# The opening of an image tower's mixer in its own instruction order, and the class token's gates and routing moved

## Time and profile before

| | |
|---|---|
| Median of 3 runs | 1067.86 us (1067.56 to 1068.58) |
| The profiled execution | 1067.47 us, its span 1065.7 us |
| Busy share of the span | TensorE 91%, VectorE 66%, ScalarE 43%, GpSimd 35% |
| Mean granted TensorE clock | 0.955 |
| Steps 0 to 3 and step 4 up to its shared expert | 0 to 132 us |
| The rest of the mixer's steps | 132 to about 608 us |

### The profile page before, as it was taken

The page is one execution under the profiler, slowest core; times in us unless marked ns, Lnnn a source line. Parts: engine busy times, 40 slices in busy tenths (PEclk is TensorE's granted clock), DMA queues, the critical chain, the costliest instruction groups (busy, mean ns, idle before and its releaser), DMA issues.

```text
span 1065.7 us, 21605 instructions
## 1 busy us (share of the span) xinstructions
PE 970.7 (91%) x6889; PEld 899.1 (84%) x6890; DVE 705.3 (66%) x2095; ACT 454.7 (43%) x1139; POOL 378.0 (35%) x468
## 2 busy tenths in 40 slices
PE   5787788999999999999788999999999999999995
PEld 3555587888888888888787899999999999999995
DVE  3458788887887877888776446464645546564643
ACT  2011143344444444444332255555555555555553
POOL 4232554242343243343421133443243424243222
PEclk9667799999999999999999799999999999999998
DMA  9300610111100111100011372837272633664322
GB/s 275 104 10 11 173 40 1 40 42 40 40 20 22 38 40 40 40 20 15 32 45 41 122 202 45 208 52 190 40 212 45 168 79 80 163 129 126 45 40 31
DMA packets 48164, 82.68 MB, mean 78 GB/s; under 512 B 6416, under 2 KB 30883, under 8 KB 48132
## 3 DMA queue, kind: packets, MB, share of 16 engines
q0 software_dynamic: 31056, 57.46, 22.3%
q1 hardware_dynamic: 17076, 24.84, 7.9%
HBM read 55.32 MB, written 26.96 MB: 77 GB/s over the span
## 4 chain that ended last, share of the span: by engine, by line
PE 41%; issue 27%; DVE 15%; POOL 13%; ACT 1%; POOLq 1%; DMA 0%; DVEq 0%; SPq 0%; ACTq 0%
PE ps_nd L657 14%; PE ps_proj L642 8%; POOL out L603 5%; PE ps_proj L722 5%; PE ps_ri L642 4%; DVE rden L1254 3%; PE ps_ip L642 3%; POOL v_rows L498 2%; PE ps_nd L843 2%; POOL h L561 1%; PE ps_h L830 1%; PE ps_h L815 1%; POOL rstd L494 1%; PE ps_t L729 1%; DVE A L1386 1%
## 5 line engine op out<-in xcount | busy, mean ns | idle before, releaser
L1077 DVE TENSOR_TENSOR GL<-g_act,GH 128x256 fp32r<-128x256 f32 (+1 forms) x424 | 185.3, 439 | 189.4 <-ACT GH L955 170.3
L657 PE MATMUL ps_nd<-w2h,GH 128*128 128x256 f32 x832 | 248.9, 299 | 24.9 <-DVE GL L1077 13.5
L950 ACT ACTIVATE g_act<-ps_proj,fcb 128x256 f32<-128x256 f32 (+1 forms) x280 | 130.8, 468 | 308.8 <-PE ps_proj L642 300.6
L657 PE MATMUL ps_nd<-w2l,GH 128*128 128x256 f32 x832 | 235.8, 283 | 0.0
L657 PE MATMUL ps_nd<-w2h,GL 128*128 128x256 f32 x832 | 234.7, 282 | 0.0
L657 PEld LDWEIGHTS ps_nd<-w2h,GH 128*128 128x128 f32 x832 | 158.4, 190 | 35.2 <-DVE GL L1077 14.0
L955 ACT CAST GH<-g_act 128x256 fp32r<-128x256 f32 x416 | 161.4, 397 | 0.0
L657 PEld LDWEIGHTS ps_nd<-w2l,GH 128*128 128x128 f32 x832 | 158.8, 191 | 0.0
L657 PEld LDWEIGHTS ps_nd<-w2h,GL 128*128 128x128 f32 x832 | 158.1, 190 | 0.0
L642 PE MATMUL ps_proj<-xh,w1h 128*128 128x256 f32 x544 | 116.3, 295 | 9.3 <-issue 4.4
L603 POOL DMA_INDIRECT out<-yb,rows_to x72 | 114.8, 1595 | 16.7 <-issue 12.8
(11 more groups left out here) (271 smaller groups left out, 1943.4 us busy)
## 6 DMA issues: line engine op xcount, KB each, us to landing
R<-v_rows SPq DMA_DIRECT2D x37, 260.0 KB
w1h<-fc_w POOLq DMA_DIRECT2D x9, 1024.0 KB
w2h<-pj_w POOLq DMA_DIRECT2D x9, 1024.0 KB
stage<-fc_w POOLq DMA_DIRECT2D x9, 1024.0 KB
stage<-pj_w POOLq DMA_DIRECT2D x9, 1024.0 KB
v_rows<-tail_rows SPq DMA_DIRECT2D x16, 260.0 KB, 3.0
x<-x SPq DMA_DIRECT2D x16, 256.0 KB, 3.6
out<-yb SPq DMA_DIRECT2D x16, 256.0 KB, 2.1
```

Source lines behind the costliest of these rows:

```text
L657: last = pe.matmul(banks[a], g[:, j, a * P:(a + 1) * P], w[i][:, j, :], start=(j == 0 and q == 0), stop=(j == HT - 1 and q == 2))
L950: act.activation(g_act[:, j % G_SLOTS, 0:width], banks[j % len(banks)][:, 0:width], ACT.Gelu_apprx_tanh, bias=fcb[i][:, j:j + 1]).then_inc ...
L1077: dve.tensor_tensor(GL[:, j, 0:width], g_act[:, j % G_SLOTS, 0:width], GH[:, j, 0:width].bitcast(F32), ALU.subtract).then_inc(gl_done, 1)
```

## The change

Steps 0 to 3 no longer use `step` but a function `opening` of each engine, with an order of their own. The parts of step became functions with names, and step calls them in the same order as before. In `steps`:

```diff
-        def steps(step):
+        def steps(opening, step):
             def over(eng):
                 for t in range(PEEL):
-                    step(t, t % 2)
+                    (opening if t < DEPTH - 1 else step)(t, t % 2)
```

ScalarE's opening follows the same order (tanh of the gates ahead of the projections' copies of steps 2 and 3). The class token's gates, in cls_a of TensorE, in fp32 on the weights as loaded:

```diff
-                pe.wait_ge(gate_w_split, 6)
-                pe.wait_ge(cls_dve, 4)
+                pe.wait_ge(gate_w_loaded, 48)
+                pe.wait_ge(cls_act, 1)
                 for i in range(3):
                     for e in range(FT):
-                        dst = ps_ri[:, i // 2, ((i % 2) * FT + e) * 2:((i % 2) * FT + e) * 2 + 2]
-                        last = split_product(pe, dst, (gates_h[i], gates_l[i]),
-                                             slice(e * P, (e + 1) * P), (c_uh, c_ul))
+                        c = (i % 2) * FT + e
+                        for k in range(FT):
+                            last = pe.matmul(ps_ri[:, i // 2, c:c + 1],
+                                             gates_raw[i][:, k, e * P:(e + 1) * P], c_ut[:, k:k + 1],
+                                             start=(k == 0), stop=(k == FT - 1))
```

```diff
                 if live(t - 4):
                     n = t - 4
+                    if isinstance(n, int) and n == 1:
+                        cls_d()
                     pe.wait_ge(vl_done, n + 1)
-                    pe.wait_ge(run_ready, n + 1)
+                    if not (isinstance(n, int) and n == 0):
+                        pe.wait_ge(run_ready, n + 1)
```

More of the change, by code:

```diff
@@ L391, in step @@
                     store_base(sp, t - 5)
-            return step
+            return opening, step
         def experts_sync(sp):
@@ L664, in mixer_tensor, with columns @@
         def mixer_tensor(pe):
-            def columns(row, dst):
+            def columns(row, dst, copies):
                 for k in range(FT):
-                    for c in range(2):
-                        last = pe.matmul(dst[:, 2 * k + c:2 * k + c + 1],
+                    for c in range(copies):
+                        last = pe.matmul(dst[:, copies * k + c:copies * k + c + 1],
                                          row[0:1, k * P:(k + 1) * P], ones_pp[0:1, 0:1],
@@ L782, in ranks, with transpose_y, scan_out @@
                 last.then_inc(rank_ready, 1)
+            def transpose_y(n):
+                if isinstance(n, int) and n == 0:
+                    pe.wait_ge(consts, CONSTS)
+                pe.wait_ge(y_ready, n + 1)
+                after(pe, ul_done, n)
+                transposes(Y).then_inc(yT_ps, 1)
+            def scan_out(n):
+                if isinstance(n, int) and n == 0:
+                    pe.wait_ge(cls_row1, 1)
+                pe.wait_ge(scan_done, FT * (n + 1))
+                pe.wait_ge(hx_done, at_most(n + 2, NIMG))
+                for lt in range(LT):
+                    for k in range(FT):
+                        last = pe.matmul(ps_h[:, lt, :], HS[:, k, lt * P:(lt + 1) * P],
+                                         wout_sb[:, k, :], start=(k == 0), stop=(k == FT - 1))
+                last.then_inc(attn_ready, 1)
@@ new lines, in y_out @@
+            def y_out(n):
+                if isinstance(n, int) and n == 0:
+                    pe.wait_ge(w_loaded, 16 * W_LOADS)
+                pe.wait_ge(yT_sb, n + 1)
+                after(pe, h1_done, n - 1)
+                for lt in range(LT):
+                    for f in range(FT):
+                        last = pe.matmul(ps_h[:, lt, :], YT[:, f, lt * P:(lt + 1) * P],
+                                         outw_sb[:, f, :], start=(f == 0),
+                                         stop=(f == FT - 1))
+                    last.then_inc(h_ready, 1)
@@ new lines, in numerators @@
+            def numerators(n):
+                if isinstance(n, int) and n == 0:
+                    pe.wait_ge(prep_act, 1)
+                pe.wait_ge(ekv_done, LT * (n + 1))
+                after(pe, t1_done, LT * n)
+                after(pe, y_done, 2 * (n - 4))
+                for tt in range(LT):
+                    for s in range(LT):
+                        last = pe.matmul(ps_nd[:, tt, :], ewT[:, s, tt * P:(tt + 1) * P],
+                                         E[:, s, :], start=(s == 0), stop=(s == LT - 1))
+                    last.then_inc(nd_ready, 1)
@@ L809, in step @@
                 if live(t - 3):
[L810 to L817, removed]
+                    scan_out(t - 3)
                 if live(t):
@@ L820, in step @@
                 if live(t - 1):
[L821 to L833, removed]
-                if live(t):
[L835 to L845, removed]
+                    y_out(t - 1)
+                if live(t):
+                    numerators(t)
                 n = t - 4
@@ L1001, in step @@
                 if live(t - 1):
[L1002 to L1010, removed]
+                    copy_y(t - 1)
                 if live(t):
                     exp_and_tanh(t, par, 1)
[L1013 to L1016, removed]
                 if live(t - 4) and live(t):
@@ L1404, in step @@
                 shared(t - 4, range(6, 7))
                 if live(t - 2):
[L1406 to L1411 removed]
+                    scan(t - 2)
                 shared(t - 4, range(7, 8))
```

490 lines of the change are left out of this document (314 added, 176 removed).

## The result

| | before | changed |
|---|---|---|
| Median, us | 1067.71 (1067.48 to 1068.58, 4 runs) | 1059.03 (1057.70 to 1060.27, 4 runs) |
| Ratio | | 0.9915, 95% interval 0.9902 to 0.9929 |
| The profiled execution | 1067.47, span 1065.7 | 1057.70, span 1055.9 |
| First matmul of the shared expert, step 4 | 131.99 | 113.43 |
| The same, step 5 | 167.00 | 157.16 |

Faster by 8.7 us where 3.5 were forecast, and 0.5 us outside the range. In the profiled pair the opening gained 18.56 us (12.9 forecast), and 8.7 of them went again between the end of step 4's products and step 5's shared expert (9.4 forecast). The remaining 9.8 us stay nearly whole to the end.

What follows compares the result with a forecast made beforehand. TensorE bounds the kernel from 132 to 560 us, waits bound the opening. Opening -12.9 and class routing between steps 4 and 5 +9.4 give -3.5 us: 1064.4 beside 1067.86; range 1059.5 to 1070.5, the forecast's own 1062 to 1067.

Steps and rivals of the forecast that it cites:

- the opening: First 132 us, up to step 4's shared expert: bound by waits, to be shortened by 12.9 us.
- The new chain: Steps 1 to 3 reordered: older image's U ahead of younger's numerators; step 4's transposes at 109.1 instead of 118.95.
- The loss between steps 4 and 5: Class routing there holds TensorE's routing matmuls of image 1: 6.4 us, plus 3.0 for the low clock, 9.4 together.
- the cover: Step 1: class gates and project(1,1) lie beside the making of U(0), at 39.6; gates 2.7 us, at most 5.6.
- rival A: Step 3: scan_out(0) at full clock, 2.0 not 3.8 us, gates 2.1 not 3.4; another 3.3, 1061.1 us; chance 0.20.
- the entry into step 4: From step 4's transposes to its shared expert at full clock: 10.0 instead of 13.04 us, another 3.0 gained.
- the two stretches from residual to U: Making U of one image in the opening: 9.1 us instead of 10.55, waits behind reciprocals gone.
- B: Step 5: the clock holds over the class pause; 3.0 us more gain, 1061.4 us; chance 0.08.
- C: Step 3's numerators don't bring back the full clock; the 3.0 us at step 4's entry stay, 1067.4; chance 0.08.
- E: TensorE stays at 1.2 GHz through step 2, from step 1's numerators on; 7.6 us later, 1072.0; chance 0.12.
- D: Step 1's class gates take 10.4 us; U(0) and all behind it 5.7 later, 1070.1 us; chance 0.06.

Runs made afterwards that it cites:

- 2 + 8 + 8 + 3: Changed kernel with unused 512-column matmuls: 2 in step 1 before U(0), 8 in each wait for U(1) and U(2), 3 in step 5; ratio 0.9859 to before.
- 8 + 8: Changed kernel with 8 unused 512-column matmuls in each of the two stretches where TensorE waits for U(1) and U(2); ratio 0.9845 to before.
- 8 + 8 + 3: Changed kernel with 8 unused matmuls in each wait for U(1) and U(2), and 3 in step 5 behind the class token's total; ratio 0.9849 to before.
- The filler: Unused 512-column matmuls added to the changed kernel in TensorE's waits; 16 in each of two waits left 32 records in 13.90 us, time 1070.68 us.
- old-order run: Changed kernel with the order of steps 0 to 3 as before on every engine, class token's work left in its new place; ratio 0.9959 to before.

## Why the prediction was wrong in size

**What held.** The new chain went as written: output product at 26.90, U's transposes at 38.24, 62.42 and 93.46 (39.6, 65.0 and 98.9 forecast), step 4's transposes waiting for Y(3). The loss between steps 4 and 5 was 8.7 us for 9.4: 6.1 of chain, then the low clock (2.5). From step 5 on all was earlier by 9.5 to 9.8 us. The gate matmuls took the 2.7 us of the forecast by luck: its 0.23 was a record at the low clock, and a one-column matmul leaves two records (the 12 left 24), so at that clock it would have been some 5.5 us. The full clock halved it (0.11 a record). Both stay under the cover, so nothing hung on it. The chain's links and place are shown by the runs with fewer links and with the chain elsewhere, and the order's share of the gain by the run without it.

**The step that failed** is the clock within the numerators after each wait for U. The prediction left six of their eight records at the low rate, 6.1 to 6.5 us in all. They took 4.86, 4.71 and 4.56, because the clock was full again after the first few. The same group stood in the trace of the kernel before, also out of a wait, in 5.16:

```profile
17.08 5.16 PE L843 MATMUL ps_nd<-E,ewT 128*128 128x512 f32 x8 [1.56 <-DVE E L1247]
```

The earlier trace rows has its first four records (3.46), so the other four took 1.7; the prediction added 2.6 for them. From U to Y it forecast 9.8 to 10.2 us, and 8.8, 8.65 and 8.5 were measured, 4.2 less in the three steps. The shorter numerators account for all of it: the prediction's own form, the end of the numerators plus 2.7 for Y, gives 0.3 us less than was measured in each step. The 0.3 is VectorE's, which the chain of waits shows: it takes its two halves of 1.76 and 1.66 one behind the other from the first half of the numerators on, and the second half of the numerators lies beside the first of these. In step 1 Y(1) (47.03) wasn't on the path at all; TensorE reached its transposes at 47.93, behind the gates and the projection. The run with 2 + 8 + 8 + 3 shows the term from the other side: with the clock up the numerators take 3.60 in all three steps.

Three more stretches were shorter than the working had them. The output product of image 0 ran at the full clock (1.97 us, not 3.8; 1.4 us in the start of U(0)). From Y(1) to the end of image 1's product it took 4.6 us, not 5.5. From Y(2) to the end of image 2's product it took 11.6, not 13.6: scan_out(0) began at the full clock and fell from it on the way (2.88 us, with 1.00 granted in 70 to 72 and 0.60 in 72 to 74), which is rival A in part and 1.4 of the 2.0. The gates behind it took 3.2 of the 3.4 forecast. Against these 8.5 us stand 1.4 at the entry into step 4, which I had put at the full clock. It fell there (3.46 for scan_out(1)), where TensorE had waited 1.23 us for Y(3). In the 8 + 8 run it stayed up behind the same wait of 1.23, in the one with 8 + 8 + 3 it fell; what decides that stays open. And 1.3 went to the two stretches from residual to U, for the reason in the last section. Together that is the 5.7 us by which the shared expert came earlier than forecast (119.1), to 0.1.

Some of it isn't the change's: in the second profile of the same kernel the output product of image 0 ran at the low clock (26.85 3.26), the shared expert began at 115.96 and the span was 3.0 us longer. By that profile the opening gained 16.0 us, and 9.4 of them went again. The median of 1059.0 lies 1.3 above the profiled execution for such reasons.

**The rivals.** A came in part; its own terms (1.8 and 1.3) add up to 3.1 us, not 3.3. B didn't come in the changed kernel (clock 0.52 in 144 to 146), but the run with 2 + 8 + 8 + 3 shows what it is worth, 2.6 us (18.0 beside 20.6). C came in part: the clock was full again for Y(3)'s transposes (0.66), but fell at the scan product behind them. E didn't come: in 44 to 46 us the clock was at 1.00. D's price didn't come, but my argument against it was wrong. The filler shows that an fp32 matmul leaves two records, so its 512 columns take 0.87 us at the full clock, and per column 3.6 times an fp32r matmul's (0.12 for 256), not 1.9 times. The Trainium skill (FP8 and Floating Point Precision, TensorE Precision Notes) states four passes; the trace comes near that for wide operands. For one column it doesn't: at the full clock an fp32 matmul took 0.22 us and an fp32r one of two columns 0.11, a factor of two.

## What to carry to other kernels

Where TensorE waits on a path, price what follows at the clock that follows: 14 us of unused matmuls in two waits were worth some 7 us, nearly what the whole change brought, and 28 us of them, which outlast the waits, took back all that the change had gained. Before pricing a group by a rate, look for the whole group in the trace: here it stood there, 1 us shorter than the sum. A chain of small dependent instructions cost its links (0.21 us each) between steps 4 and 5, and in the two other places tried, where the engine that runs it feeds the bound, its idle share made no room for it either.

## What the runs showed of the hardware that was not expected

**VectorE's scan and GpSimd's adds slow each other.** In the new order they fall together, in steps 2 and 3. VectorE and GpSimd, step 3:

```profile
87.11 2.34 DVE L1438 TENSOR_TENSOR_SCAN HS<-A,c_h,S 128x256 f32<-128x256 f32 x2
```

```profile
87.28 1.64 POOL L569 TENSOR_TENSOR h<-h,lng_bc 128x512 f32<-128x512 f32 x1 [0.85 <-DVE h L1195]
```

Apart, the two scans take 1.39 us together (in the old-order run, at 78.25) and the add 1.27. This goes with the 0.65 us by which each stretch from residual to U was longer than forecast. The Trainium skill (SBUF — State Buffer, Who interferes with whom) states that a VectorE operation with two SBUF inputs and a GpSimd operation that reads SBUF share a port pair, which one holds as a lock for its whole instruction. The scans and the adds, both longer only where they meet, agree with that. So does a small instruction of step 1 in the changed kernel:

```profile
32.68 1.27 POOL L569 TENSOR_TENSOR h<-h,lng_bc 128x512 f32<-128x512 f32 x1 [0.95 <-DVE h L1195]
32.81 1.16 DVE L1271 SCALAR_TENSOR_TENSOR c_s<-c_g,c_om 128x2 f32<-128x2 f32 x1
```

In the kernel before it takes 0.16 us. Here it begins 0.13 us behind the add and ends within 0.02 us of it.

**The clock fell behind a wait in one execution and held behind the same wait in another.** Near the end of step 4 TensorE waits for a low part (GL): 2.82 us in the changed kernel's first profile, 2.88 in its second, 2.86 in the run with 8 + 8 + 3. TensorE alone, the last of these, then the first:

```profile
130.00:132.00 2.00, 1.23 (x6) 0.50 0.00 0
132.00:134.00 2.00, 2.00 (x11) 0.50 0.37 133
134.00:136.00 2.00, 2.00 (x11) 0.50 0.19 67
```

```profile
132.00:134.00 2.00, 1.90 (x15) 1.00 0.18 67
```

With 8 + 8 + 3 the clock went to 0.50 behind the wait and stayed there while TensorE was busy all of the time from 132 to 136 us; it was back in 136 to 138 (0.83). In the changed kernel's second profile it went down too (0.50 in 134 to 136), in its first it stayed at 1.00. Such differences, here and at the output product of image 0, make 3 us between two profiles of one kernel, nearly as much as was forecast for the whole change.
